# Four masks, a split fold and two queues: one edit set at the seam between a graph kernel's second and third layer

## The chip, the cores and the metric

The kernel runs on one core of one Trainium2 chip. The metric is the device time of one launch in microseconds (us). The kernel before took 700.03 us (median of three executions, 698.61 to 701.37).

## What is computed

Four pre-norm graph layers over 4096 nodes with 64 features. `adj` is a dense 4096 by 4096 float32 matrix with many zeros. Each layer is `x = x + L(relu(layernorm(x)), adj)`:

```
layer 0:  1 - 0.1 h - 0.01 sum(h * (adj @ h))
layer 1:  two hops  h = tanh([adj @ h, h] @ W[k])
layer 2:  w @ (h @ weight) + bias;  w keeps the last 100 nonzeros of each
          row of adj, weighted 0.5 ** (distance from the row's last one)
layer 3:  MLP(h) + adj @ (h B^T) - rowsum(adj) * (h B^T)
```

## The kernel before

The work is five passes over `adj`: `L0`, `L1A` (first hop), `L1B` (second hop), `L2`, `L3`. Each pass has 8 chunks of 512 output nodes, and each chunk 16 blocks (`b` = 0 to 15) of 1024 columns. Two consecutive blocks are a pair, 1 MB, which is the unit of a load. 15 of the 64 pairs stay in `cache`; all others are loaded again in every pass into one of the six slots of `land`. Neighbouring passes run over the chunks in opposite orders or end on the chunk where the next begins, so that the pairs in the slots serve twice at a seam: the last chunk of `L1B` and the first of `L2` are the same.

TensorE (PE) does two float32 matmuls per block in `L0`, `L1A`, `L1B` and `L3` (line 1373). In `L2` it does, per block, a triangle matmul on a 0/1 mask (`triangle`, line 1408), which gives each entry's rank as an exponent, and three blocks later (`LAG`) the weighted sum (`weigh`, line 1424). VectorE (DVE) makes the masks six blocks ahead (`LEAD`; `mask`, line 1155). ScalarE (ACT) turns ranks into weights (`weights_out`, line 591), except for blocks 3 and 13 of a chunk, which DVE does (line 589). Row 127 of each mask pair is not made by DVE: a small DMA brings it from `counts` (`counts_for`).

The row sums of `adj`, needed in `L3`, are gathered on DVE beside the hops: blocks in `TOTALS` are added up (lines 1107, 1111), and at a chunk's last such block `fold_totals` transposes and reduces them in two halves (lines 1138, 1139), through the tile `tS`. The total of the last `L1B` chunk lies in the uS places that masks 6 and 7 of `L2` will use, so those masks, and the counts rows for them (`counts_for(3)`, on SyncE's queue), wait until it is folded (semaphore `folded`).

What is done with a finished chunk, its epilogue, is cut into stages, and each engine runs stage k after the block that a table names: `STAGES_L1A`, `STAGES_L1B`, `STAGES_L2`, and `QUICK` for a pass's first chunk, which closes the pass before. For a chunk of `L1B` the stages go: ACT copies the sums out (line 850); PE joins two halves (line 1267); DVE adds the hop's own term ("added", line 1007) into `tS`; ACT does tanh (line 865) into `natS`; DVE adds the residual and centres the rows (3: lines 1075, 978, 979); GpSimd (POOL) squares (line 769); DVE makes the variance (4: lines 984, 985); POOL makes the inverse root (line 762) and scales (line 772); DVE takes the relu (5: line 997), which gives `hS`; PE transposes ("turn", line 1236); ACT copies to `rowsT` (line 830); PE multiplies by the layer-2 weight (6: line 1289); ACT copies back (8: line 883); POOL splits the rows in high and low parts (lines 795, 797). SyncE sends one row of the low part to another tile (`left_rows_of`, line 651), and the last matmul of an `L2` chunk (line 1432) needs it.

In `L2` the epilogue is similar: PE joins (line 1254), DVE adds (line 1082), and after the relu PE transposes (line 1276), ACT evacuates to `rowsT` (line 830), PE multiplies (line 1286). `rowsT` is also stored in DRAM as `rows_transposed` for `L3`, by SyncE's queue (`keep_rows`, line 656), and ACT doesn't overwrite `rowsT` before this store has landed (`hT_out`).

SyncE's queue runs in order. It carries all the loads of `adj`, each behind waits for the slot's last users, and between them the small DMAs: `after_masks` decides behind which load each goes. At the start of `L2`:

```
if p == L2 and c == 0:
    counts_for(2)
    sp.wait_ge(left_out, 16 * NC)
    left_over(0)
    left_over(1)
    counts_for(3)
```

After the last chunk of `L3`, `finish` runs three stages once more: ACT copies the sums (line 850), PE joins (line 1267), DVE adds the side term (line 1097), ACT's queue stores.

## Time and profile before

| | us |
|---|---|
| three executions | 698.61, 700.03, 701.37 |
| the profiled execution, its own time | 700.7 |
| its span, first to last instruction's end | 698.9 |
| PE busy | 668.3 (96%) |
| DVE busy | 469.6 (67%) |
| ACT busy | 192.5 (28%) |
| POOL busy | 114.2 (16%) |

The profile is one execution. A duration of an instruction is its own; "idle before" is the time in which its engine did nothing, with what ended that. PEld is the weight load of PE, which lies under the matmul before it. SPq and ACTq rows are the issues of DMAs. Of a DMA the time from issue to landing is given where the profile has it.

In time the passes lie as follows: `L0` to about 195 us, `L1A` to 311, `L1B` to 426.7, `L2` to 562, `L3` to the end.

### The profile page before, as it was taken

The page shows a single profiled execution, that of the slowest core. Times are in us where ns is not written, and L with a number is a line of the kernel's source. Part 1 is how long each engine was busy: PE and PEld are TensorE (multiplying, and loading weights), DVE is VectorE, ACT ScalarE, POOL GpSimd, SP SyncE. Part 2 cuts the span into 40 slices and gives each one's busy share as a digit, 9 for nine tenths or more (in the row PEclk, how much of TensorE's full clock was granted, in tenths as well). Part 3 has the DMA queues.
Part 4 walks back from the last instruction along what each step waited for, and adds up shares of the span by engine and source line. Part 5 has one row for each costly group of instructions (what it writes and reads, how often), then busy time and mean ns, then how long its engine had stood idle before and what let it go on. Part 6 is the DMA issues. An engine that isn't in the chain of part 4 may idle for free.

```text
span 698.9 us, 10418 instructions
## 1 busy us (share of the span) xinstructions
PE 668.3 (96%) x3811; PEld 270.2 (39%) x3824; DVE 469.6 (67%) x813; ACT 192.5 (28%) x296; POOL 114.2 (16%) x132
## 2 busy tenths in 40 slices
PE   3999999999999999999999998899999999999997
PEld 1434433334433333333344443444444443333332
DVE  7777767777899999996888888899989810000000
ACT  1101111011111001101111116899998811111111
POOL 4110011110200000001222223222332211211111
PEclk9999999999999999999999999999999999999999
DMA  8999999998589999959999983999999479999992
GB/s 347 422 410 411 413 412 409 418 414 335 190 329 388 420 422 419 415 206 402 384 406 420 419 368 134 362 378 408 414 414 412 191 263 341 417 415 418 417 419 98
DMA packets 42098, 256.51 MB, mean 367 GB/s; under 512 B 5120, under 2 KB 11264, under 8 KB 11840
## 3 DMA queue, kind: packets, MB, share of 16 engines
q1 hardware_dynamic: 38712, 252.85, 89.6%
q10 hardware_dynamic: 3336, 3.00, 1.5%
q8 instruction: 31, 0.51, 0.3%
q14 instruction: 19, 0.16, 0.1%
HBM read 252.28 MB, written 3.54 MB: 366 GB/s over the span
## 4 chain that ended last, share of the span: by engine, by line
PE 53%; DMA 20%; DVE 19%; POOL 4%; issue 3%; ACT 0%; SPq 0%; DVEq 0%; ACTq 0%; POOLq 0%
PE accA L1373 37%; DMA cache<-adj_blocks 10%; DVE uS L1111 8%; DMA land<-adj_blocks 6%; PE accA L1424 4%; PE work L1408 4%; DVE uS L1155 3%; POOL rstd L762 2%; DMA rows_transposed<-rowsT 2%; PE work L1391 1%; PE work L1336 1%; POOL tS L772 1%; PE accA L1342 1%; PE work L1267 1%; PE work L1304 1%
## 5 line engine op out<-in xcount | busy, mean ns | idle before, releaser
L1373 PE MATMUL accA<-land,X 128*64 128x512 f32 x1568 | 374.1, 598 | 13.6 <-DVE X L1197 11.3
L1373 PEld LDWEIGHTS accA<-land,X 128*64 128x64 f32 x1568 | 110.6, 137 | 193.7 <-issue 166.9
L1155 DVE TENSOR_SCALAR uS<-land 128x1024 bf16<-128x1024 f32 (+1 forms) x196 | 134.5, 730 | 30.1 <-DMA land<-adj_blocks 28.4
L1111 DVE TENSOR_TENSOR uS<-uS,land 128x512 f32<-128x512 f32 x178 | 125.2, 704 | 9.6
L1373 PE MATMUL accA<-cache,X 128*64 128x512 f32 x480 | 120.1, 598 | 2.6 <-DMA cache<-adj_blocks 2.6
L591 ACT ACTIVATE wS<-work 128x1024 uint16<-128x1024 f32 x114 | 109.2, 1037 | 8.8 <-PE work L1408 8.7
L769 POOL TENSOR_TENSOR hS<-tS 128x256 f32<-128x256 f32 x24 | 23.5, 978 | 400.5 <-DVE tS L979 400.5
L1097 DVE TENSOR_TENSOR zS<-uS,work 128x256 f32<-128x256 f32 x8 | 3.4, 421 | 123.1 <-PE work L1267 106.9
L1408 PE MATMUL work<-uS,triA 128*128 128x512 bf16 x248 | 74.4, 380 | 2.2 <-DVE uS L1155 1.8
L1424 PE MATMUL accA<-wS,X 128*128 128x512 bf16 x251 | 74.7, 379 | 0.3
L850 ACT ACTIVATE accS<-accA 128x512 f32<-128x512 f32 x32 | 19.1, 598 | 177.3 <-PE accA L1373 165.5
L1373 PEld LDWEIGHTS accA<-cache,X 128*64 128x64 f32 x480 | 35.0, 138 | 59.4 <-issue 54.8
L1391 PE MATMUL work<-uS,later 128*64 128x512 bf16 x256 | 49.1, 379 | 0.0
L1155 DVE TENSOR_SCALAR uS<-cache 128x1024 bf16<-128x1024 f32 (+1 forms) x60 | 39.8, 686 | 7.1 <-DMA cache<-adj_blocks 6.9
L762 POOL TENSOR_TENSOR rstd<-var,power 128x4 f32<-128x4 f32 (+1 forms) x25 | 34.0, 1360 | 34.7 <-DVE var L985 34.7
L1424 PEld LDWEIGHTS accA<-wS,X 128*128 128x128 f16 x256 | 25.0, 98 | 30.0
L1408 PEld LDWEIGHTS work<-uS,triA 128*128 128x128 bf16 x256 | 23.8, 101 | 26.3 <-DVE uS L1155 5.0
L1111 DVE TENSOR_TENSOR uS<-uS,cache 128x512 f32<-128x512 f32 x46 | 31.8, 691 | 2.5
L1391 PEld LDWEIGHTS work<-uS,later 128*64 128x64 bf16 x256 | 16.4, 110 | 35.5 <-issue 27.1
L997 DVE TENSOR_SCALAR hS<-tS 128x256 f32<-128x256 f32 x24 | 10.0, 416 | 27.1 <-POOL tS L772 27.1
L830 ACT ACTIVATE rowsT<-work 128x256 f32<-128x256 f32 x15 | 5.8, 384 | 70.0 <-PE work L1236 70.0
L782 POOL TENSOR_TENSOR uS<-X,rowsum 128x256 f32<-128x256 f32 x8 | 4.9, 613 | 100.4 <-DMA xin<-x_rows 78.4
(109 smaller groups left out, 417.4 us busy)
## 6 DMA issues: line engine op xcount, KB each, us to landing
land<-adj_blocks SPq DMA_DIRECT2D x221, 1024.0 KB, 10.3
cache<-adj_blocks SPq DMA_DIRECT2D x15, 1024.0 KB, 16.7
xin<-x_rows ACTq DMA_DIRECT2D x8, 128.0 KB, 7.6
out_rows<-zS ACTq DMA_DIRECT2D x8, 128.0 KB, 6.9
uS<-counts ACTq DMA_DIRECT2D x60, 4.0 KB
x_rows<-zS SPq DMA_DIRECT2D x7, 128.0 KB, 11.4
rows_transposed<-rowsT SPq DMA_DIRECT2D x7, 128.0 KB, 8.6
wS<-rows_transposed SPq DMA_DIRECT2D x7, 128.0 KB, 8.5
```

The lines of the kernel that those rows point to most:

```text
L591: ops.activation(w, of, ACT.Relu).then_inc(w_ready, 1)
L762: nc.gpsimd.tensor_tensor(out[:, 0:ntile], of[:, 0:ntile], power[:, 0:ntile], ALU.pow)\
L769: nc.gpsimd.tensor_tensor(hS[:, :], tS[:, :], tS[:, :], ALU.mult).then_inc(rows_squared, 1)
L772: nc.gpsimd.tensor_tensor(rows4(tS), rows4(tS), spread(rstd[:, 0:4]), ALU.mult).then_inc(rows_scaled, 1)
L850: last = nc.scalar.activation(accS[:, :], accA[:, c % 2, :], ACT.Copy)
L997: nc.vector.tensor_scalar(to, tS[:, :], 0.0, float(np.sqrt(D)), ALU.max, ALU.mult).then_inc(h_ready, 1)
L1111: nc.vector.tensor_tensor(total, total, of[:, i * W:(i + 1) * W], ALU.add)\
L1155: nc.vector.tensor_scalar(masks(p, c, b)[0:rows, :], block_of(p, c, b)[0:rows, :], 0.0, None, ALU.not_equal)\
L1373: last = nc.tensor.matmul(accA[k * D:(k + 1) * D, c % 2, :], tile(X[p % 2], TQ * q + k), of[:, k * W:(k + 1) * W], start=(b == 0), stop=(b ...
L1391: last = nc.tensor.matmul(spare[k * D:(k + 1) * D, c % 2, :], later[:, NT - t:NT - t + D], masks(L0, c, b)[:, k * W:(k + 1) * W], start=(b ...
L1408: last = nc.tensor.matmul(work[:, 2 * (n % TRI_PAIRS) + k, :], triA[:, :], masks(L2, c, b)[:, k * W:(k + 1) * W], start=True, stop=True)
L1424: last = nc.tensor.matmul(accA[:, c % 2, :], tile16(TQ * q + k), weights(n)[:, k * W:(k + 1) * W].bitcast(BF16), start=(b == 0 and k == 0) ...
```

## The change

1. DVE makes masks 0 to 3 of `L2`'s first chunk in the last chunk of `L1B`, after blocks 10, 12, 13 and 14 (`MASKS_AHEAD`).
2. At the start of `L2`, DVE's order is: mask 4, "added", mask 5, stage 3, first half of the fold, variance, second half of the fold, sum of the two parts. Before it was: masks 0 and 1, both halves and the sum, "added", masks 2 and 3, stage 3, masks 4 and 5, and the variance after the first block. The last fold goes through `zS` in place of `tS`.
3. PE does the join of the last `L1B` chunk after the second triangle of `L2`, no longer ahead of the first. The other quick stages come one or two blocks earlier.
4. In `L1A` "added" and tanh come one block earlier; in `L1B` the relu (5) comes after block 11, not 10.
5. The store of `rowsT` is issued by ACT right behind the copy that fills it, and no longer by SyncE.
6. The end of the kernel is done in two halves, each with its own copy, join, add and store.

```diff
+MASKS_AHEAD = {10: 0, 12: 1, 13: 2, 14: 3}
...
-STAGES_L1A = {1: 2, "added": 4, "tanh": 6, "hop": 8, "hopped": 10}
+STAGES_L1A = {1: 2, "added": 3, "tanh": 5, "hop": 8, "hopped": 10}
...
-STAGES_L1B = {1: 3, "added": 5, "tanh": 6, 3: 7, 4: 8, 5: 10, "turn": 12, "turned": 13, 6: 14, 8: 15}
+STAGES_L1B = {1: 3, "added": 5, "tanh": 6, 3: 7, 4: 8, 5: 11, "turn": 12, "turned": 13, 6: 14, 8: 15}
...
-         L2: {"tanh": 0, 4: 0, 5: 2, "turn": 8, "turned": 9, 6: 10, 7: 10, 8: 11,
-              "row sums": 14},
+         L2: {"tanh": 0, "join": 1, 5: 1, "turn": 7, "turned": 7, 6: 9, 8: 9,
+              "row sums": 12},
...
 def last_stages(before):
-    return [(k, before) for k in SUM_STAGES]
+    return [("last " + k, before) for k in SUM_STAGES]
...
+        def last_nat(h):
+            return (nat, tr)[h][:, 0:2 * D]
+
+        def last_half(t, h):
+            return t[:, h * 2 * D:(h + 1) * 2 * D]
...
-            def keep_rows(c):
-                sp.wait_ge(tr_evac, tr_no(L2, c) + 1)
-                sp.dma_start(hT_d[ch(L2, c)], rowsT[:, :]).then_inc(hT_out, 16)
...
-                if issued["keep"] < NC - 2 and g >= PAIRS * (issued["keep"] + 2) + 2:
-                    keep_rows(issued["keep"])
-                    issued["keep"] += 1
...
                     rows_transposed(p, c)
+                    if p == L2 and c < NC - 1:
+                        act.wait_ge(tr_evac, tr_no(p, c) + 1)
+                        act.dma_start(hT_d[ch(p, c)], rowsT[:, :]).then_inc(hT_out, 16)
...
+                if at == "last sums":
+                    act.wait_ge(intra_done, c + 1)
+                    act.wait_ge(swept, sweep_no(p, c) + 1)
+                    act.wait_ge(nat_done, nat_no(p, c))
+                    for h in range(2):
+                        nc.scalar.activation(accS[:, h * CH:(h + 1) * CH], accA[:, c % 2, h * CH:(h + 1) * CH], ACT.Copy)\
+                            .then_inc(acc_evac, 1)
+                if at == "last store":
+                    for h in range(2):
+                        act.wait_ge(nat_evac, nat_no(p, c) + 1 + h)
+                        act.dma_start(last_half(chunk(out, ch(p, c)), h), last_half(zS, h)).then_inc(rows_out, 16)
...
+                if (p, c) == (L1B, NC - 1) and b in MASKS_AHEAD:
+                    mask(L2, 0, MASKS_AHEAD[b])
...
-                for h in range(2):
+                by = zS if (p, c) == (L1B, NC - 1) else tS
+                for h in halves:
                     at = (2 * k + h) * 8
-                    L(nc.vector.transpose(tS[:, :], totals(k)[:, h * CH:(h + 1) * CH]))
+                    L(nc.vector.transpose(by[:, :], totals(k)[:, h * CH:(h + 1) * CH]))
...
                 if p == L2 and c == 0:
-                    for b in range(2):
-                        mask(p, c, b)
-                    fold_totals(L1B, NC - 1)
-                    nc.vector.tensor_tensor(part_sums, part_sums, more_sums, ALU.add).then_inc(folded, 1)
+                    mask(p, c, len(MASKS_AHEAD))
                     epilogue("added", before)
-                    for b in range(2, 4):
+                    for b in range(len(MASKS_AHEAD) + 1, LEAD):
                         mask(p, c, b)
                     epilogue(3, before)
-                    for b in range(4, LEAD):
-                        mask(p, c, b)
+                    fold_totals(L1B, NC - 1, halves=(0,))
+                    epilogue(4, before)
+                    fold_totals(L1B, NC - 1, halves=(1,))
+                    nc.vector.tensor_tensor(part_sums, part_sums, more_sums, ALU.add).then_inc(folded, 1)
...
-                if p != L2 and at == ("sums" if p == L3 else 1):
+                if p != L2 and at == ("sums" if p == L3 else "join" if (p, c) == (L1B, NC - 1) else 1):
```

PE's "last sums" waits for each half of ACT's copy, joins it with eight matmuls into `last_nat(h)`, and DVE's "last result" adds each half as it is done.

## Rows read from the trace of the kernel before

**Rows 1.** The page: GB/s moved by DMA in 40 slices of the span.

```profile
GB/s 347 422 410 411 413 412 409 418 414 335 190 329 388 420 422 419 415 206 402 384 406 420 419 368 134 362 378 408 414 414 412 191 263 341 417 415 418 417 419 98
```

**Rows 2.** Windows: length, busy PE, PEld, DVE, ACT, POOL, clock, DMA, GB/s.

```profile
335.20:413.70 78.50, 76.50 (x483) 33.26 (x481) 65.48 (x121) 8.91 (x20) 18.44 (x25) 1.00 1.01 413
...
426.75:449.93 23.18, 18.59 (x118) 7.94 (x120) 20.43 (x38) 19.69 (x24) 7.93 (x8) 1.00 0.83 305
449.93:465.92 15.99, 15.60 (x79) 7.93 (x80) 13.90 (x23) 14.10 (x17) 3.97 (x4) 1.00 0.99 379
...
530.10:547.30 17.20, 15.88 (x78) 7.70 (x79) 15.11 (x26) 13.90 (x18) 3.94 (x4) 1.00 1.01 416
```

**Rows 3.** Timeline, first hop: start, duration, engine, line, idle before.

```profile
202.96 0.68 DVE L1060 SCALAR_TENSOR_TENSOR countS<-lowS,rowsT 32x512 uint16<-32x512 f32 x1
...
204.23 0.71 PE L1304 MATMUL work<-wts,rowsT 64*128 64x128 f32 x8 [0.88 <-ACT rowsT L865]
```

**Rows 4.** Timeline of PEld: the join in chunks of the second hop.

```profile
320.16 0.14 PEld L1267 LDWEIGHTS work<-wts,accS 128*64 128x64 f32 x2 [0.28 <-issue]
...
335.23 0.14 PEld L1267 LDWEIGHTS work<-wts,accS 128*64 128x64 f32 x2 [0.28 <-issue]
...
413.67 0.17 PEld L1267 LDWEIGHTS work<-wts,accS 128*64 128x64 f32 x2 [0.26 <-issue]
```

**Rows 5.** Second hop: PE's and DVE's waits (total, times, longest), and loads.

```profile
PE work L1236 <- DVE hS L997: 2.6, 6, 0.6
...
DVE hS L997 <- POOL tS L772: 12.7, 7, 1.8
...
L753 SPq DMA_DIRECT2D land<-adj_blocks x31: 327/328/437, 335.8 to 408.8; - x31
...
DMA to landing us min/median/max: 6.8/9.3/11.6
```

**Rows 6.** Timeline of the second hop's last chunk and of L2's first.

```profile
422.63 0.29 DVE L997 TENSOR_SCALAR hS<-tS 128x256 f32<-128x256 f32 x1 [1.81 <-POOL tS L772]
422.84 1.41 DVE L1111 TENSOR_TENSOR uS<-uS,land 128x512 f32<-128x512 f32 x2
...
425.69 1.29 DVE L1155 TENSOR_SCALAR uS<-land 127x1024 bf16<-127x1024 f32 x2
...
428.75 0.22 SPq L634 DMA_DIRECT2D uS<-counts  x1
...
434.38 0.59 PE L1408 MATMUL work<-uS,triA 128*128 128x512 bf16 x2
...
449.62 0.37 PE L1432 MATMUL accA<-lowS,later 32*128 32x512 bf16 x1 [1.57 <-DMA later<-X]
```

**Rows 7.** Loads in L2 at 456:471 and 520:535; a DVE wait.

```profile
DMA to landing us min/median/max: 7.1/8.4/10.3
...
DMA to landing us min/median/max: 12.6/14.7/15.7
...
545.91 1.30 DVE L1155 TENSOR_SCALAR uS<-land 127x1024 bf16<-127x1024 f32 x2 [1.08 <-DMA land<-adj_blocks]
551.43 0.42 DVE L1082 TENSOR_TENSOR zS<-X,accA 128x256 f32<-128x256 f32 x1 [0.69 <-PE accA L1254]
```

**Rows 8.** Stores of rows: L2, then L3 (issue to landing last); ACT and PE.

```profile
rows_transposed<-rowsT SPq DMA_DIRECT2D x5, 128.0 KB, 12.0
...
out_rows<-zS ACTq DMA_DIRECT2D x5, 128.0 KB, 6.9
...
543.53 0.38 ACT L830 ACTIVATE rowsT<-accA 128x256 f32<-128x256 f32 x1 [2.74 <-DMA rows_transposed<-rowsT]
544.06 0.68 PE L1286 MATMUL accA<-wts,rowsT 128*128 128x128 f32 x4 [1.09 <-ACT rowsT L830]
```

**Rows 9.** Timeline of the end.

```profile
694.67 0.60 ACT L850 ACTIVATE accS<-accA 128x512 f32<-128x512 f32 x1 [11.41 <-PE accA L1373]
...
696.59 0.34 ACTq L614 DMA_DIRECT2D out_rows<-zS  x1
```

More of the change, by code:

```diff
@@ L679, in _ @@
             LEFT_ROWS_AT = {NC - 3: 1, NC - 2: 3, NC - 1: 7}
-            issued = {"keep": 0, "left": 2, "left rows": NC - 3}
+            issued = {"left": 2, "left rows": NC - 3}
             def step(p, c, before, before2):
@@ L697, in step @@
                     after_masks(PAIRS * NC - 1)
-                    keep_rows(NC - 2)
                 if p == L0:
@@ L948, in finish @@
                     epilogue(k, e)
-                act.wait_ge(rows_out, 16 * 2 * NC)
+                act.wait_ge(rows_out, 16 * (2 * NC + 1))
             for g in range(1, PRO_GROUPS):
@@ L1091, in epilogue @@
                     side = sideS[:, (c % 2) * CH:(c % 2 + 1) * CH]
+                    if at == "last result":
+                        dve.wait_ge(side_ready, c + 1)
+                        rows_written()
+                        for h in range(2):
+                            dve.wait_ge(nat_done, nat_no(p, c) + 1 + h)
+                            nc.vector.tensor_tensor(last_half(zS, h), last_half(side, h), last_nat(h), ALU.add)\
+                                .then_inc(nat_evac, 1)
                     if at == "result":
@@ L1124, in main, with fold_totals @@
                     weights_out(dve, nc.vector, c, b)
-            def fold_totals(p, c):
+            def fold_totals(p, c, halves=(0, 1)):
                 k = ch(p, c)
@@ L1257, in epilogue @@
                         last.then_inc(nat_done, 1)
-                if p != L2 and at == ("sums" if p == L3 else 1):
+                if at == "last sums":
+                    nat_free(nat_no(p, c, 0))
+                    for h in range(2):
+                        pe.wait_ge(acc_evac, NC * p + c + 1 + h)
+                        for j, at, half in pieces(4)[4 * h:4 * h + 4]:
+                            last = nc.tensor.matmul(last_nat(h)[half, (j % 2) * D:(j % 2 + 1) * D], accS[:, at:at + D], wt("join"),
+                                                    start=True, stop=True)
+                        last.then_inc(nat_done, 1)
+                    return
+                if p != L2 and at == ("sums" if p == L3 else "join" if (p, c) == (L1B, NC - 1) else 1):
                     nat_free(nat_no(p, c, 0))
@@ L1435, in step @@
             def step(p, c, before, before2):
-                for k, e in early_stages(p, c, before, before2):
-                    epilogue(k, e)
                 s = NC * p + c
```

4 lines of the change are left out of this document (1 added, 3 removed).

## The prediction

> **What bounds the kernel now.** I read the waits first, then windows by pass, then the timeline of the seam at 427 us, then the landing times of the loads. PE is busy 96% of the span, so only what PE waits for, or what sets its pace, can be gained. Three resources run close together. In the second hop the DMA share is 1.01 and 413 GB/s are moved [rows 2], against a best slice of 422 [rows 1]: about 2% is left there. In the first hop DMA is as full (420 to 422 in its slices [rows 1]). In L2 it starts empty (0.83, 305 GB/s in the first chunk) and is full at the end (1.01, 416) [rows 2]; a load there lands 8.4 us after its issue early on and 14.7 us late [rows 7]. The backlog grows while PE, at 16.0 us a chunk, isn't hurt yet. The reader should keep this in mind: what PE gains before L2 must be matched by the loads in L2.
>
> Places where PE loses time, and which the edits touch:
>
> - Second hop: PE waits for the relu `hS` six times, 2.6 us [rows 5]. The join comes 15.07 us after the one before in the first chunk, which has no such wait, and then 78.44 us for five chunks (335.23 to 413.67), 15.69 each [rows 4]. So a chunk loses 0.62, more than the wait shown, since the weight loads ahead are no longer hidden. What makes `hS` late is DVE's own loop: it stands idle 12.7 us in seven chunks, 1.8 each, for POOL's scaling [rows 5], with sums still to do.
> - First chunk of L2: 23.18 us against 15.99 for the next [rows 2], with 1.57 us of wait for the small DMA ahead of line 1432 [rows 6].
> - The chunk 530.1 to 547.3: 17.20 us [rows 2]. ACT waits 2.74 us until the earlier store of `rowsT` has landed, PE then 1.09 [rows 8].
>
> **Part by part.** All in us, gains negative.
>
> *Relu after block 11 (second hop).* The sums of block 11 (1.41 [rows 6]) move into DVE's idle 1.81, and the relu still starts when POOL is done, at 422.63 in the row. DVE's loop falls from 15.65 to about 14.24, under PE's 15.07. So each of the five chunks gains 0.62: -3.1. If loads hold it back, less: 31 loads were issued from 335.8 to 408.8 and land 6.8 to 11.6 later, median 9.3 [rows 5]. The last one, pair 1 of the last chunk, is thus in by about 418.1 (415.6 to 420.4). DMA can come forward by some 1.5 at most (2% of 78.5).
>
> *Four masks in that chunk.* Mask 0 is made after block 10 and needs just that pair 1. DVE's queue stands still until it has landed, and behind it are the sums of block 11 and the relu. The old relu ended at 422.92 [rows 6] with PE waiting 0.6 for it; with PE 3.1 earlier, the turn would want `hS` at 419.2. With the landing at 418.1 it is ready at 418.1 + 0.65 (a mask is half of line 1155's 1.29 for two [rows 6]) + 1.41 + 0.29 = 420.5. PE waits 1.3, where it waited 0.6. I take 0.8 off the gain: second hop -2.3, bounds -1.0 (landing as late as the row allows) and -3.7 (all waits gone).
>
> *Start of L2.* PE needn't wait for ACT's copy nor for masks 0 to 5: three triangles run at once. But masks 6 and 7 and their counts rows wait for the fold, and the fold moves behind "added", stage 3 and the variance. Counted from the second hop's end T (426.75 before [rows 2]): join done T + 1.6 (two triangles and the join), "added" 2.1 (0.42, as line 1082 has for the same size [rows 7]), mask 5 2.7, stage 3 (three such instructions and a wait for tanh) 4.1. Both halves of the fold and the sum took from the end of the first two masks, 426.98, to the issue at 428.75 [rows 6], so half a fold takes 0.85: 5.0. The variance waits for POOL's square, an estimated 1.0 (the idle 1.81 holds two POOL steps [rows 6]): 5.9, half a fold and the sum 6.8. SyncE's `counts_for(3)` was issued at 428.75 [rows 6], which is T + 2.0; now it goes at T + 6.8. It lands some 2 later, and triangle 6 starts at T + 8.8; before it was 434.38 - 426.75 = T + 7.6 [rows 6]. So PE stands idle before triangle 6 and is 1.2 behind. What gives it back: the turn, layer-2 weight and row split come one and two blocks earlier, the row leaves for line 1432 at about T + 16.5 and is in before PE is there. From triangle 6 to line 1432 PE took 449.62 - 1.57 - 434.38 = 13.7 before [rows 6], with some waits for ACT in it that I put at 0.7, so 13.0 now: T + 21.8 against 449.62 - 426.75 = T + 22.9. Sum -1.0, rounded; bounds +0.5 (counts 1.5 later) and -1.6 (nothing but the 1.57 of wait).
>
> *What is queued behind that wait.* `counts_for(3)` holds SyncE's queue, and behind it are all the loads for L2's second chunk. They were first issued right behind it, at 429.1; with T 2.3 earlier (424.4) they now start at 431.5, three at once. So PE comes 3.3 earlier to the second chunk and the loads start 2.4 later. They catch up, since before they were spaced by waits for slots: I count a pace of 2.6 each from the first landing, 436.4, which puts the sixth at 449.4, and about 1.3 more from later gaps that close. Loads in L2 end up some 2.2 earlier than before, PE wants to be 3.3 and later 4.8 earlier.
>
> *Store of rowsT by ACT.* It no longer stands behind 1 MB loads in SyncE's queue. There it took 12.0 to land, the same size from ACT's queue in L3, with the loads at 417 GB/s, 6.9 [rows 8]. It is also issued at once. The chunk at 530.1 falls from 17.2 to the usual 16.0, 0.3 of start-up apart: -1.5 (bounds 0 and -1.5). The cost: ACT waits for its own copy and issues, some 0.4 per chunk. It lies in the time in which ACT has nothing to do (busy 14.10 of 15.99 in a chunk [rows 2]), next to block 13, whose weights DVE makes. Without that cover it would be 7 x 0.4 = 2.8.
>
> The Trainium skill, "DMA: Bandwidth & Descriptors", section "Queues, rings and completion order", says that each DMA engine takes turns between the queues it has work for. By that the store alternates with the loads, as 6.9 beside 12.0 suggests. The same page, "Issuing engines are not separate DMA queues", says that a second issuer saves only issue time, which speaks against any more bandwidth; by it the loads gain nothing here and the sum stays.
>
> *Give-back in L2.* At 545.91 DVE waits 1.08 for a load and, five masks and a weight later, still has 0.69 of idle before line 1082 [rows 7], from where the chain to `hS` and the turn is tight. So the loads may come 0.7 later against PE than they did, and no more. With loads 2.2 earlier, PE can be 2.9 earlier at the end of L2, where the edits alone would give -2.3 - 1.0 - 1.5 = -4.8. Give-back +1.9, bounds 0 (DMA recovers all) and +3.5 (loads not earlier at all).
>
> *First hop.* "Added" was never late there but once: PE waited 0.88 at 204.23 [rows 3]. ACT's tanh was then released by line 1060 (202.96 to 203.64), which shares `rowsT` and stays where it is, with as much DVE work ahead as before. 0; at most +0.4, as the sums of a block end 0.41 later.
>
> *The end.* From 694.67 to the last store's issue at 696.59 is 1.92 [rows 9]. In halves, copy, join and add overlap: the second half's add is half as long and the join of the first lies under the second copy, at two short copies of 0.38 [rows 8] for one of 0.60. -0.3; bounds +0.1 and -0.5. The last store is half as big; the row bounds what that is worth by the 2.3 from its issue to the span's end, most of which I expect to stay. The Trainium skill, same page, "Anatomy of one DMA", fits a DMA from GpSimd's queue by about 2.0 and its bytes at 436 GB/s, which is 2.3 for these 128 KB, as in the trace; by that the smaller store would bring an estimated 0.15 more than my sum has.
>
> **Sum.** -2.3 - 1.0 - 1.5 + 1.9 + 0 - 0.3 = -3.2. The profiled execution had 700.7 with a span of 698.9, so 697.5 and 695.7. The median stands 0.7 below that execution: 700.0 - 3.2 = 696.8.
>
> **Rivals.**
>
> 1. *Loads keep up* (chance 0.25). For it: in the first 40 us of L2 the loads had gaps, and the stores leave SyncE's queue. Against: 416 GB/s at the end. Then no give-back: 700.0 - 4.8 - 0.3 = 694.9.
> 2. *The late fold costs what the masks bring* (0.20). Loads aren't earlier at all, give-back +3.5, or the last chunk of the second hop waits for pair 1: -4.8 + 3.5 - 0.3 = -1.6: 698.4.
> 3. *Slower: counts behind the store in ACT's queue* (0.07). The counts rows for blocks 6 and 7 of the next chunk are issued after block 15, right after the store, and their triangle runs seven blocks later, at 16.0 a chunk about 7.0. If they come only after the store has landed, it decides whether that takes more than 7. With the 6.9 of rows 8 it just doesn't. At 9.5 it costs 2.5 in each of six chunks, +15: 700.0 - 3.2 + 15 = 712. From 8 us on the change is slower.
> 4. *My forecast*: 0.48.
>
> **How the numbers follow.** About 0.5% (3.5 us) is what a measurement of this kernel can tell from no change. My case lies at 696.8 with its own range 695.5 to 698.0, so it is split by 696.5: 0.2 faster, 0.28 same. Faster is 0.25 + 0.2 = 0.45, same 0.28 + 0.20 = 0.48, slower 0.07. The range goes from 694.3 (rival 1 with somewhat more of the hop) to 699.0 (rival 2 with the bounds of the fold).
>
> **What would show it.** Joins in the second hop 15.07 apart; no PE wait on `hS` except in the last chunk, and there a DVE wait for a load at mask 0; `counts_for(3)` some 6.8 after the hop's end and PE idle before triangle 6; no wait at line 1432; no ACT wait for `rows_transposed`; chunks of L2 that grow from 16.0 at the start to more than 16.3 at the end with DVE waits for loads of 2 us and more. Wrong would be: full 16.0 to the end (rival 1), hop chunks still at 15.6, or waits of triangles for counts.

## The result and the profile after

The changed kernel takes 702.97 us (median of seven runs, 701.88 to 704.47) beside 700.03 for the kernel before; the ratio is 1.0044, its 95% interval 1.0029 to 1.0059. It is slower by 2.9 us. The forecast was 696.8 with a range up to 699.0, so the result lies outside it. Of the cases in the forecast only rival 3 (0.07) lay above, at 712. The profiled run took 704.47 with a span of 702.6, which is 3.7 more than the span before.

The lines of the page of the changed kernel that answer to the table of before, and the granted clock in 40 slices of the span:

```profile
span 702.6 us, 10422 instructions
...
PE 669.2 (95%) x3810; PEld 272.3 (39%) x3824; DVE 471.9 (67%) x814; ACT 193.0 (27%) x297; POOL 120.4 (17%) x132
...
PEclk9999999999999999999999999899999999999999
```

PE has the same work. It is busy 0.9 longer (669.2 beside 668.3) and idle 2.8 longer; where it is busy longer, its clock was low, as the second chunk of L2 below shows. One slice of the clock, from 439 to 457 us, is not full; before, none was short. POOL is busy 6.2 us longer with the same instructions.

The windows of the changed kernel, in the columns of [rows 2] (length, busy PE, PEld, DVE, ACT, POOL, clock, DMA share, GB/s): five chunks of the second hop, L2 from the end of the hop to line 1465 (which is line 1432 of before), the next chunk, and the slow chunk late in L2.

```profile
334.84:412.07 77.23, 76.48 (x483) 33.77 (x481) 67.03 (x120) 8.90 (x20) 23.61 (x25) 1.00 1.01 413
425.76:450.71 24.95, 17.97 (x115) 7.73 (x118) 17.95 (x34) 19.92 (x24) 7.42 (x8) 0.97 0.70 284
450.71:469.17 18.46, 18.26 (x79) 8.84 (x80) 13.58 (x22) 13.34 (x16) 3.97 (x4) 0.86 0.88 332
533.53:550.48 16.95, 15.87 (x79) 7.98 (x80) 15.39 (x24) 14.41 (x18) 4.18 (x4) 1.00 1.02 416
```

The hop gained 1.2 over five chunks where the prediction wanted 3.1. The first chunk of L2 took 24.95; from the same point, the end of the hop, to the same matmul it was 22.84 before. The second chunk has the same work as before and takes 18.46 instead of 16.01, at a clock of 0.86. Cut at the same events, the two spans part like this:

| stretch | before | after | change |
|---|---|---|---|
| start to the first join of the second hop (J) | 320.16 | 319.42 | -0.74 |
| J to the end of the second hop | 106.59 | 106.34 | -0.25 |
| end of the hop to the left row of L2's first chunk | 22.84 | 24.95 | +2.11 |
| second chunk of L2 | 16.01 | 18.46 | +2.45 |
| six more chunks of L2 | 96.22 | 96.67 | +0.45 |
| from there to the first `intra` matmul of L3 | 17.39 | 17.43 | +0.04 |
| rest | 119.69 | 119.37 | -0.32 |

The first row needs care: 0.72 of the 0.74 are there already at 189 us, before any edited stage has run, and in the changed kernel and those below J lies between 317.25 and 319.42. So stretches are compared from J on.

Timeline of the changed kernel at the seam (start, duration, engine, line, and in brackets the idle time before and what ended it):

```profile
427.44 0.42 DVE L1024 TENSOR_TENSOR tS<-wS,accA 128x256 f32<-128x256 f32 x1 [1.77 <-issue]
...
429.63 0.44 DVE L1165 STREAM_TRANSPOSE zS<-uS 128x256 f32<-128x256 f32 x1
...
431.57 0.42 DVE L1166 TENSOR_REDUCE wts<-zS 128x8 f32<-128x256 f32 x1
432.02 0.22 SPq L646 DMA_DIRECT2D uS<-counts  x1
...
432.34 0.83 SPq L756 DMA_DIRECT2D land<-adj_blocks  x2
...
433.43 0.59 PE L1441 MATMUL work<-uS,triA 128*128 128x512 bf16 x2 [2.12 <-DMA uS<-counts]
...
433.93 0.87 SPq L756 DMA_DIRECT2D land<-adj_blocks  x2
...
437.84 1.54 SPq L756 DMA_DIRECT2D land<-adj_blocks  x2
...
441.80 0.60 SPq L663 DMA_DIRECT2D later<-X  x1
...
446.09 0.59 PE L1457 MATMUL accA<-wS,X 128*128 128x512 bf16 x2
...
450.74 0.58 PE L1465 MATMUL accA<-lowS,later 32*128 32x512 bf16 x1 [4.06 <-DMA later<-X]
```

And the six loads that are issued from 432 to 440, from issue to landing:

```profile
DMA to landing us min/median/max: 4.7/10.1/11.9
```

Read it from the top. DVE is idle for 1.77 before "added", since it waits for the join; the fold, which before the change stood in that place, comes only at 429.63 and ends at 431.99. The counts rows leave at 432.02, 6.3 after the hop's end (before: 2.0 [rows 6]). Two things follow from that one issue. PE is idle for 2.12 before triangle 6. And the loads of the second chunk, which stand behind the counts rows in SyncE's queue, leave in a bunch: the first four, whose slots are free, in 2.1 us, all six in 6.7. Before, the six went out over 12.3 us, from 429.1 to 441.4, and landed in 4.9 to 9.3; now it is up to 11.9. The small DMA with the last row is issued at 441.80 behind them, when four of them are still on their way, and is in at about 450.7. Before, it was issued at 445.32 with two on their way, and was in at about 449.6. PE has finished its last block at 446.7 and waits 4.06. During this wait, at 449.04, the chip's clock for TensorE falls to its 1.2 GHz level (0.5 in the record) for 6.83 us, and PE does the first part of the second chunk at half speed. The mean granted clock is 0.994 or 0.995 in all seven executions of the changed kernel, and the fall accounts for that.

The last chunk of the second hop in the changed kernel, where mask 0 is made ahead:

```profile
419.13 0.69 DVE L1182 TENSOR_SCALAR uS<-land 127x1024 bf16<-127x1024 f32 x1
419.30 1.38 POOL L765 TENSOR_TENSOR rstd<-var,power 128x4 f32<-128x4 f32 x1 [1.16 <-DVE var L1002]
419.74 1.41 DVE L1135 TENSOR_TENSOR uS<-uS,land 128x512 f32<-128x512 f32 x2
420.76 0.85 POOL L775 TENSOR_TENSOR tS<-tS,rstd 128x256 f32<-128x256 f32 x1
421.65 0.29 DVE L1014 TENSOR_SCALAR hS<-tS 128x256 f32<-128x256 f32 x1 [0.50 <-POOL tS L775]
...
422.09 0.66 PE L1260 MATMUL work<-wts,hS 128*64 128x128 f32 x8 [1.20 <-DVE hS L1014]
```

Mask 0 waited for no load, which the prediction had feared. PE's wait of 1.20 came from POOL, which was late instead. Without the masks ahead (e4_no_seam below) it is 0.96 in the same place, against 0.58 before the change, so most of the lateness isn't the masks'.

### The profile page after: what moved, and what is told of

Read it like the earlier page. It is cut to its first block, busy times and chain, and to the rows that moved or that the text cites. A ratio compares the mean times of both kernels' runs of the same rounds, so it can differ in the third digit from the quotient of the medians.

```text
span 702.6 us, 10422 instructions
## 1 busy us (share of the span) xinstructions
PE 669.2 (95%) x3810; PEld 272.3 (39%) x3824; DVE 471.9 (67%) x814; ACT 193.0 (27%) x297; POOL 120.4 (17%) x132
## 4 chain that ended last, share of the span: by engine, by line
PE 54%; DMA 22%; DVE 15%; POOL 4%; issue 4%; ACT 0%; SPq 0%; DVEq 0%; ACTq 0%; POOLq 0%
PE accA L1406 38%; DMA cache<-adj_blocks 10%; DMA land<-adj_blocks 10%; DVE uS L1135 7%; PE work L1441 4%; PE accA L1457 4%; POOL rstd L765 2%; DVE uS L1182 2%; PE work L1424 1%; DMA later<-X 1%; PE work L1369 1%; PE work L1300 1%; POOL tS L775 1%; PE accA L1375 1%; PE work L1260 1%
## 5 line engine op out<-in xcount | busy, mean ns | idle before, releaser
L1135 DVE TENSOR_TENSOR uS<-uS,land 128x512 f32<-128x512 f32 x178 | 127.5, 716 | 9.3
```

The source lines that it names most:

```text
L1135: nc.vector.tensor_tensor(total, total, of[:, i * W:(i + 1) * W], ALU.add)\
```

## The experiments

Fourteen kernels, each timed in five rounds against the kernel before on the same chip. The last three columns are from the profiled run of each: from J to the left row of L2's first chunk, the second chunk, and the six after it. Before has 129.43, 16.01, 96.22; the changed kernel 131.29, 18.46, 96.67. The comparisons were made on several chips, where the kernel before had medians of 699.5 to 700.0, so a difference between two medians of this table is good to some tenths; the ratios allow for that.

| kernel | median | ratio to before | J to left row | 2nd chunk | six more |
|---|---|---|---|---|---|
| e4_no_seam | 697.31 | 0.9966 (0.9955 to 0.9978) | 127.25 | 16.00 | 96.65 |
| e11_late_fold | 704.58 | 1.0057 (1.0037 to 1.0078) | 133.09 | 18.49 | 96.12 |
| e9_fold_first | 697.63 | 0.9968 (0.9955 to 0.9980) | 127.94 | 16.01 | 96.87 |
| e12_fold_first_kept | 696.76 | 0.9949 (0.9929 to 0.9970) | 127.26 | 16.00 | 96.50 |
| e1_left_by_act | 700.08 | 1.0004 (0.9991 to 1.0016) | 128.76 | 16.00 | 98.52 |
| e2_counts_by_act | 698.71 | 0.9987 (0.9974 to 1.0000) | 130.47 | 15.99 | 96.20 |
| e8_both_by_act | 699.81 | 0.9994 (0.9978 to 1.0010) | 131.27 | 15.99 | 96.22 |
| e3_filler | 701.69 | 1.0031 (1.0019 to 1.0044) | 132.76 | 15.99 | 95.72 |
| e13_fold_first_left_by_act | 697.64 | 0.9964 (0.9949 to 0.9979) | 128.18 | 16.00 | 96.59 |
| e5_store_by_act | 699.45 | 0.9998 (0.9985 to 1.0011) | 129.20 | 16.01 | 96.90 |
| e6_relu11 | 698.47 | 0.9983 (0.9969 to 0.9997) | 127.47 | 16.00 | 97.21 |
| e14_turn_later | 693.66 | 0.9902 (0.9881 to 0.9923) | 124.69 | 16.00 | 96.34 |
| e15_masks_ahead_turn_later | 696.06 | 0.9945 (0.9928 to 0.9962) | 126.04 | 16.01 | 96.12 |
| e16_changed_turn_later | 701.15 | 1.0012 (0.9995 to 1.0028) | 129.23 | 18.63 | 96.68 |

### Without the seam edits: e4_no_seam

The kernel before with the hop orders, the store by ACT and the two-part end; masks, fold, join and `QUICK[L2]` as before.

> The kernel before with only the three edits away from the seam: the relu after block 11 in the second hop and added/tanh a block earlier in the first, the store of rowsT by ACT, and the two-part end. Theory A: nothing of the loss, since the masks, the fold and the counts are where they were; second hop 1.2 faster over five chunks, the chunk at 530 about 0.5 to 1.4 faster, the end 0.3: 698.0 to 699.0, clock 1.00. If these edits carry the loss (ACT's queue with the store in it, or the relu): 701 or more.

697.31, faster than before. By the ratios the rest of the change brings 2.4 us; the seam edits (masks ahead, early join, late fold, earlier stages) turn 0.9966 into 1.0044 and so cost 5.5. The kernel is faster than the 698.0 to 699.0 expected.

### The late fold alone: e11_late_fold

```diff
                     for b in range(2):
                         mask(p, c, b)
-                    fold_totals(L1B, NC - 1)
-                    nc.vector.tensor_tensor(part_sums, part_sums, more_sums, ALU.add)...
                     epilogue("added", before)
...
                     for b in range(4, LEAD):
                         mask(p, c, b)
+                    fold_totals(L1B, NC - 1)
+                    nc.vector.tensor_tensor(part_sums, part_sums, more_sums, ALU.add)...
```

This is e4_no_seam with the fold moved, and through `zS`, as in the change.

> The kernel with edits 4 to 6 alone (697.3), with one more edit: the fold goes behind the added sum, stage 3 and masks 4 and 5 in VectorE's order; no mask is made ahead, and the stages of L2's start stay where they were. Theory A (the late fold alone makes the loss): counts rows at 5 us or more after the hop's end, PE idle 1.5 or more before triangle 6, loads in a bunch of four or more within 3 us, the one-row DMA late by 2 or more, and 701 to 703 in all. Theory B (the late fold hurts only together with the early masks and stages, since PE otherwise comes as late as the counts): 697 to 699.

704.58: 7.3 more than e4_no_seam (6.4 by the ratios), the slowest of all, and above the 701 to 703 of theory A. Timeline of this kernel:

```profile
433.39 0.22 SPq L640 DMA_DIRECT2D uS<-counts  x1
...
434.89 0.59 PE L1436 MATMUL work<-uS,triA 128*128 128x512 bf16 x2 [2.17 <-DVE uS L1174]
...
445.57 0.60 SPq L657 DMA_DIRECT2D later<-X  x1
...
452.26 0.58 PE L1460 MATMUL accA<-lowS,later 32*128 32x512 bf16 x1 [3.86 <-DMA later<-X]
```

The whole picture is there without any mask made ahead: counts late, PE idle before triangle 6 (what comes last there is mask 6, which waits for the fold too), the row late, a second chunk of 18.49.

### The fold first again: e9_fold_first and e12_fold_first_kept

The changed kernel with the order of the fold put back, all else kept:

```diff
                     mask(p, c, len(MASKS_AHEAD))
+                    fold_totals(L1B, NC - 1)
+                    nc.vector.tensor_tensor(part_sums, part_sums, more_sums, ALU.add)...
                     epilogue("added", before)
...
-                    fold_totals(L1B, NC - 1, halves=(0,))
                     epilogue(4, before)
-                    fold_totals(L1B, NC - 1, halves=(1,))
-                    nc.vector.tensor_tensor(part_sums, part_sums, more_sums, ALU.add)...
```

> The changed kernel with one thing put back: both halves of the fold and the sum stand ahead of the added sum in VectorE's order (as before the change), while four masks are still made ahead and the stages come early. Theory A (the late fold is the seam's whole loss): VectorE is idle 1.8 us there, waiting for the join, so the fold costs nothing; counts rows go out some 2 us after the second hop's end and not 6.3, PE has no idle time ahead of triangle 6 (2.1 less), the loads are no longer issued in a bunch, the one-row DMA lands within 3 us, PE waits at most 1 for it and the clock stays at 1.0: 696.5 (695.5 to 697.5), level with the kernel that has no seam edits (697.3) or just under it. Theory B (the early masks and the earlier stages cost by themselves, or the last row is late whatever the loads do): PE still waits 3 or more at the row and the time stays at 700 or above.

e9_fold_first transposes into `zS`, which still holds the kept rows of the last chunk until stage 3 has added them, so in this kernel the fold's values take their place and the rows of that chunk are lost. Its instructions and their order are those of e12_fold_first_kept, which folds through `tS` and keeps them.

> The changed kernel with the fold ahead of the added sum again, through the tile tS as before the change, so that the kept rows of the last chunk survive. Same operations, order and waits as the kernel with the fold first that gave 697.6: both theories expect 697.6 within 0.7, so that this is a repetition; more than 1.5 above it would mean that the tile matters.

697.63 and 696.76, so the place of the fold in VectorE's order is worth 5.3 and 6.2 us; from J to the first `intra` matmul it is 6.7 in the profiled runs (257.14 against 263.85). In the timeline of e12_fold_first_kept:

```profile
425.91 0.22 SPq L646 DMA_DIRECT2D uS<-counts  x1
...
426.23 0.83 SPq L756 DMA_DIRECT2D land<-adj_blocks  x2
...
440.21 0.60 SPq L663 DMA_DIRECT2D later<-X  x1
...
445.14 0.37 PE L1464 MATMUL accA<-lowS,later 32*128 32x512 bf16 x1 [1.32 <-DMA later<-X]
```

The six loads land in 4.8 to 8.8 here instead of 4.7 to 11.9, the row is issued with two of them on their way and needs less than 5 instead of 9, and no clock is lost. Theory A of e9_fold_first holds in mechanism; 697.63 is just above its range.

### What goes through the row and what through the loads: e1, e2, e8, e3

e1_left_by_act: the changed kernel, last one-row DMA by ACT after block 12.

```diff
+                if (p, c, b) == (L2, 0, 12):
+                    act.wait_ge(copy_used, copied_no(L1B, NC - 1, 1) + 1)
+                    act.dma_start(loS[4 * NC - 4:4 * NC, :], chunk(X[1], NC - 1)[LAST:P, :]...
```

> The changed kernel, but the last of the eight one-row transfers that line 1465 waits for is issued by ACT's queue (after block 12 of L2's first chunk) and not by SyncE's. Theory A (the row stands behind six loads in SyncE's queue, PE idles 4.06 us for it, and the granted clock then falls to half for 6.8 us): the row lands within 4 us of its issue at about 442.5, PE reaches line 1465 at 446.7 and doesn't wait, the clock stays at 1.00, L2's second chunk takes 16.0 and not 18.4; 4.1 + 2.4 less, of which L2's loads take back 1 to 3: 696.5 to 699.5 against 703.0. Rival B (the loads themselves, started 3.3 us later than before, set the end of L2, and the row only hides it): the row's wait goes but L2 ends no earlier, 701 to 703.

It was issued at 440.80 on the other queue and PE waits 1.54 in place of 4.06. The clock stays at 1.0 and the second chunk at 16.00, 700.08 in all: above the 696.5 to 699.5 of theory A and below the 701 of its rival. But the loads are as late as before the edit, and the six later chunks take 98.52, 1.85 more than in the changed kernel.

e2_counts_by_act: the counts rows of masks 6 and 7 by ACT, so that loads are not queued behind them.

```diff
-                    counts_for(3)
...
+                if (p, c, b) == (L2, 0, 5):
+                    act.wait_ge(folded, SUMMED - 1)
+                    act.dma_start(*counts_of(3)).then_inc(counts_in[3], 16)
```

> The changed kernel, but the counts rows for masks 6 and 7, which wait for the fold, are issued by ACT (after block 5) and not by SyncE, so that SyncE's loads aren't held behind the fold. Theory A: loads start at about 427 to 429 as slots come free, fewer stand ahead of the row, PE's wait at line 1465 falls from 4.1 to 1 or less and the clock may stay up: 697 to 700. Rival B (late loads): the same place gains, and more than in the run with the row on ACT's queue, 696 to 698. If neither the start of the loads nor the row matters: 703.

The first three loads leave at 422.66, 424.18 and 427.58, before the counts rows (431.05). PE waits 3.79 for the counts, longer than before: with loads already on their way it is 3.1 from their issue to PE's start, against 1.4 in the changed kernel, where the counts rows go first. Just after this wait the clock falls, for 3.41 us from 434.54 on. PE doesn't wait at all for the row, and the later chunks keep 96.20. 698.71. Freeing the loads brings more than freeing the row alone.

> The changed kernel with both small DMAs taken off SyncE's queue: counts rows of masks 6 and 7 by ScalarE after block 5, the last one-row DMA by ScalarE after block 12. Each alone gave 698.7 and 700.1. Theory A (two separate losses, one from loads held back, one from the row behind a bunch of loads): counts still wait for the late fold, PE waits 2 to 4 there, but neither the row nor the clock costs: 697.5 to 698.5. Theory B (L2 is bound by DMA at its end, and what PE gains at its start goes back): no better than the better of the two, 698.7 or 0.3 around it.

e8_both_by_act has both edits. 699.81 is not better than e2_counts_by_act; theory A wanted 697.5 to 698.5. The window over the first chunk of L2, from its profiled execution (701.36, the slowest of its twelve), shows what happened there:

```profile
426.50:450.53 24.03, 19.62 (x113) 8.25 (x114) 17.94 (x34) 18.30 (x23) 4.65 (x7) 0.86 0.79 286
```

PE waits 3.6 for the counts, and the clock falls right then, from 433.49 on for 6.83 us, inside this chunk. Removing the second wait did not remove the first. The twelve executions differ in how much clock they lost: the four with a mean clock of 0.995 took 699.57 to 701.36, the two with 0.999 took 697.49 and 697.86, inside theory A's range. So where the clock stayed up, theory A's time came; but the first wait alone is enough to bring the clock down in some executions, and the median contains that. Neither theory had this.

e3_filler puts 70 matmuls of 128x128 into PE's wait for the row; nothing uses their result.

```diff
+                        pe.wait_ge(nat_evac, nat_no(L1B, NC - 1, 1) + 1)
+                        pe.wait_ge(rowsum_ready, 1)
+                        for _ in range(70):
+                            nc.tensor.matmul(accA[:, 1, 0:P], triA[:, :], triA[:, :], start=True, stop=True)
                         pe.wait_ge(left_rows, 16 * NC)
```

> The changed kernel with 70 needless 128x128 matmuls on PE ahead of the wait at line 1465, into a bank that is free, so that PE is busy while it waits for the row. Theory A's second part (it is PE's idle time of 4 us that lets the granted clock fall to half): the row is as late as ever (about 450.7), but the clock stays at 1.00 and the second chunk of L2 takes 16.0: 2.4 less, 700.5. Rival (the clock falls for another reason): clock 0.99 as before and 703.0.

The window over its second chunk:

```profile
452.02:468.01 15.99, 15.66 (x79) 7.94 (x79) 13.58 (x22) 13.33 (x16) 3.97 (x4) 1.00 0.97 348
```

With PE kept busy the clock doesn't fall there, and the same chunk takes 15.99 instead of 18.46, though the dummies end only at 452.0, 1.3 after the row was in in the changed kernel. Net it is 1.3 faster, where 2.4 had been expected. In this execution the clock fell once before the edit, at 434.48 for 3.41 us, which put PE back by some 1.5, and the dummies with it. All six executions have a mean clock of 0.997 or 0.998, against 0.994 or 0.995 in all seven of the changed kernel. So 2.45 of the loss are the clock, and PE's idle time at the row brought this fall about.

> The changed kernel with the fold first and the last one-row DMA issued by ScalarE after block 12. Theory A (PE's 1.9 of wait at that row, which is left with the fold first, is worth its length): 696.0. Theory B (loads bind the end of L2, so what PE gains at its start goes back before its end): the wait goes away, the first left-row matmul starts at 445 instead of 446.8, and the time stays within 0.5 of 697.6.

e13_fold_first_left_by_act: e12_fold_first_kept and the edit of e1. 697.64, no gain: PE waits 1.0 at the row and 1.6 for weights before it, and from J it reaches the row no earlier. Once the fold is right, the row's queue is not a lever; theory A's 696.0 did not come.

### The other parts: e5_store_by_act and e6_relu11

The kernel before with the store alone:

```diff
-SyncE: keep_rows(c), called in after_masks and at L3's start
...
                     rows_transposed(p, c)
+                    if p == L2 and c < NC - 1:
+                        act.wait_ge(tr_evac, tr_no(p, c) + 1)
+                        act.dma_start(hT_d[ch(p, c)], rowsT[:, :]).then_inc(hT_out, 16)
```

> The kernel before with the store of the transposed rows on ScalarE's queue alone. Prediction: -1.5 before give-back, with 6.9 instead of 12.0 us from issue to landing: 698.3. Rival: the chunk that had waited for the store falls from 17.2 to 17.0 only, since a load is late there too, and the next one takes it back: within 0.3 of before, 699.4 or so.

699.45, ratio 0.9998. The store of `rowsT` lands in 7.0 now (median; 6.9 in the prediction), and ACT no longer waits for it. Yet the chunk falls only from 17.49 to 17.13, and the next rises from 14.56 to 15.43. The rows of e5_store_by_act in that stretch:

```profile
528.37 1.29 DVE L1149 TENSOR_SCALAR uS<-land 127x1024 bf16<-127x1024 f32 x2 [1.29 <-DMA land<-adj_blocks]
...
537.11 1.29 DVE L1149 TENSOR_SCALAR uS<-land 127x1024 bf16<-127x1024 f32 x2 [0.36 <-DMA land<-adj_blocks]
...
540.22 0.41 PE L1270 MATMUL accA<-wts,hS 128*128 128x128 f32 x2 [1.00 <-DVE hS L991]
...
540.73 0.38 ACT L821 ACTIVATE rowsT<-accA 128x256 f32<-128x256 f32 x1 [1.42 <-PE accA L1270]
541.14 0.35 ACTq L872 DMA_DIRECT2D rows_transposed<-rowsT  x1
...
545.48 1.29 DVE L1149 TENSOR_SCALAR uS<-land 127x1024 bf16<-127x1024 f32 x2 [1.07 <-DMA land<-adj_blocks]
```

ACT's idle is now ended by PE, that is by the turn, which waits for `hS`, which waits for masks, which wait for loads: DVE's waits for loads in the last two chunks are 2.7 (1.4 before), 1.29 and 0.36 of them ahead of this turn and 1.07 in the chunk after it. The wait has only changed its name. Rival 3 of the prediction (counts behind the store in ACT's queue) did not show: no triangle waits for counts in these chunks.

The kernel before with the hop orders alone:

```diff
-L1A: {1: 2, "added": 4, "tanh": 6, ...}    L1B: {... 4: 8, 5: 10, "turn": 12, ...}
+L1A: {1: 2, "added": 3, "tanh": 5, ...}    L1B: {... 4: 8, 5: 11, "turn": 12, ...}
```

> The kernel before with the two hop orders changed alone (relu of the second hop after block 11, first hop one block earlier). Prediction's step: second hop -3.1 without the masks, joins 15.07 apart, so 697.4 after give-back. Rival (POOL's variance step takes 1.4 instead of 1.0 when it runs beside VectorE's sums, and the new order waits for the join instead): joins 15.44 apart, -1.0 to -1.3 at the hop's end, and 698.7 to 699.3 in all.

698.47, a little under the 698.7 to 699.3 of the rival. The joins stand 15.44 apart, not 15.07, as the rival had it. POOL's `rstd` in the second hop, first in the kernel before, in the changed one, and in e6_relu11 (count, then min/median/max of the duration in ns):

```profile
L762 POOL TENSOR_TENSOR rstd<-var,power x6: 1007/1009/1012, 326.6 to 405.0; 128x4 f32<-128x4 f32 x6
```

```profile
L765 POOL TENSOR_TENSOR rstd<-var,power x6: 1386/1388/1394, 325.8 to 403.0; 128x4 f32<-128x4 f32 x6
```

```profile
L762 POOL TENSOR_TENSOR rstd<-var,power x6: 1387/1388/1393, 324.8 to 402.0; 128x4 f32<-128x4 f32 x6
```

In the old order DVE was idle while POOL worked on the variance. In the new one DVE's sums run beside it, and each `rstd` takes 0.38 longer. That lies on the chain join, "added", square, variance, `rstd`, scale, relu, turn, and the chunk is just that much longer: 15.44 - 15.07 = 0.37. (PE's own waits at the turn show as 0.2 in three of the chunks.) That this chain, and not the loads, sets the 15.44 is shown by the next kernel.

The Trainium skill, "GPSIMD Engine Reference", section "Specifications", says that GpSimd's SBUF interfaces are shared with VectorE, with contention when a VectorE instruction has two SBUF inputs. The sums have two (`uS` and `land`), and the trace agrees in direction; it shows 0.38 of delay for one instruction.

### The turn one block later: e14, e15, e16

```diff
-L1B: ... 5: 11, "turn": 12, "turned": 13, 6: 14, 8: 15}
+L1B: ... 5: 11, "turn": 13, "turned": 14, 6: 15, 8: 15}
```

> The kernel with edits 4 to 6 alone (697.3), with the turn, its copy and the split of the second hop's chunks one block later. Theory A (joins stand 15.44 apart since PE, at the turn of block 12, waits 0.4 in each chunk for a chain that begins at the join of block 3: join, added, square, variance, rstd 1.39, scale, relu): with a block more the wait goes away, joins stand 15.07 apart, the hop ends 1.8 earlier, and 695.5 to 697 in all, what loads in L2 take back included. Theory B (loads set 15.44): joins stay 15.4 apart, with waits for loads in VectorE, and the time stays at 697.3.

e4_no_seam with this: 693.66, ratio 0.9902, the best kernel here: 5.9 under the kernel before and 9.3 under the changed one, between medians. It is below the 695.5 to 697 of theory A. The medians differ by 3.7 from e4_no_seam; in the profiled runs 2.9 lie between J and L3, and 1.7 before J, where the two kernels don't differ in an edited stage. The joins stand 15.07 apart in all six intervals, and `rstd` still takes 1.39, so loads did not set 15.44; the chain did. Counted from J, PE ends the hop 3.5 earlier than in e4_no_seam (some 0.6 of it because stage 6 now stands behind the last block), reaches the left row 2.6 earlier, and keeps that: the last six chunks take 96.34 (96.65 there, 96.22 before).

> The changed kernel with the fold ahead of the added sum (696.8) and the turn, its copy and the split of the second hop's chunks one block later; against the kernel with the later turn and no seam edits (693.7) it has the four masks ahead, the early join and the earlier stages of L2's first chunk. Theory A (masks ahead cost some 0.4 at the turn of the last hop chunk and give as much back at L2's start): within 0.7 of 693.7. Theory B (as in the prediction, masks ahead and early stages bring 1 us at the start of L2): 692.7 or less. Theory C (the split of the last chunk, now a block later, makes the one-row DMA late, which the early stages were to avoid): PE waits 2 or more there and 695 or more.

e12_fold_first_kept with the later turn: 696.06, 2.4 slower than e14_turn_later between medians (3.0 by the ratios). In the profiled runs 2.06 lie before J, where the two don't differ in an edited stage, so that part isn't explained. From J on the masks ahead and the early stages cost 1.35 up to the left row, where PE waits 2.4 (0.5 in e14_turn_later). Theory C comes nearest; theory B, gain from the early masks, is wrong.

> The changed kernel with nothing else than the turn, its copy and the split of the second hop's chunks one block later; the fold stays late. Theory A (the later turn gains its 3 to 4 us in the hop, in front of the seam, and the seam costs what it did): joins 15.07 apart and 699 to 700. Theory B (PE comes earlier to waits that are set by VectorE and POOL, so part of the gain goes into them): joins 15.07 apart, PE idle before triangle 6 and at the row by 1 to 2 more than in the changed kernel (2.1 and 4.1), and 701 or more.

The changed kernel with the later turn: 701.15. Theory A had 699 to 700. Its timeline:

```profile
429.79 0.59 PE L1441 MATMUL work<-uS,triA 128*128 128x512 bf16 x2 [2.23 <-DMA uS<-counts]
...
447.11 0.58 PE L1465 MATMUL accA<-lowS,later 32*128 32x512 bf16 x1 [4.07 <-DMA later<-X]
```

Joins are 15.07 apart. The waits before triangle 6 and at the row, 2.2 and 4.1, are those of the changed kernel, and the second chunk of 18.63 is nearly so. But of the 3.4 by which the hop ends earlier, counted from J, only 2.1 are left at the left row and 1.9 at L3. Some 0.6 of the difference is stage 6, which now stands behind the last block. And PE waits 0.7 for a mask at the first triangle of L2, where it waited 0.2 at most; the join stands behind that, and all that hangs on the join. The counts rows leave 7.5 after the hop's end, not 6.3. Against e14_turn_later the seam edits cost 7.5 between J and L3, where they cost 6.6 against e4_no_seam. So theory B has the time, and its mechanism in part: PE comes earlier to a wait that DVE sets, though not to one of the two that it named.

## Why the prediction was wrong, step by step

*Start of L2* is the step that failed. It said "the row leaves for line 1432 at about T + 16.5 and is in before PE is there". It left at T + 16.0 and PE was there at T + 20.9 (T + 21.8 had been forecast); the row came at T + 25.0. The issues were right within 0.6: counts at T + 6.3 (6.8) and the row; triangle 6 ran at T + 7.7 (8.8). What was missing is what the step *What is queued behind that wait* had already written down: loads that leave together. Its list of landings was used for the give-back, but not for the small DMA behind them in the same queue. By that list the sixth load landed at 449.4, and PE was to be at the row at 424.4 + 21.8 = 446.2; a row that lands with that load would have cost some 3, not nothing (it measured 4.06). The step's -1.0 measured +2.11, outside its bounds (+0.5), and the clock added 2.45, a term the sum did not have at all. [rows 6] showed the danger: the same DMA was already late by 1.57 with loads spaced out.

*Relu after block 11.* The sums do move into DVE's idle time, but the five chunks gained 1.2 and not 3.1. The term took POOL's durations from rows in which DVE was idle; the edit is what ends that idleness. DVE's loop was not the only one that PE's 15.07 had to cover; the chain through POOL was the second, 0.37 longer, and one block more of slack (e14_turn_later) removed just that. The first interval, which had none of the old wait (15.07), became 15.43 too.

*Four masks in that chunk.* -2.3 with the relu, measured -0.25, beyond the bound of -1.0. The mechanism named (mask 0 waits for a load) did not occur. The turn waited 1.20 all the same, since POOL was slower: `rstd` took 1.38, which is the relu's order again (1.39 in e4_no_seam, with a wait of 0.96), and the scale 0.85 beside a mask and sums (0.61 there). From J to the hop's end the masks cost 0.25 against e4_no_seam.

*Store of rowsT by ACT.* -1.5, measured 0 (e5_store_by_act, 0.9985 to 1.0011), which was the lower bound. The latency was right (7.0); the chunk had a second cause, a load, just behind the first. The term was also more than its own rows give: from 17.2 to 16.0 are 1.2.

*Give-back in L2.* +1.9, measured about nothing: e14_turn_later reaches the left row 4.7 earlier from J than before, and its next six chunks take only 0.12 longer. Rival 1 was right on that. The store's gain did go to loads that were late, but their lateness does not grow with PE's lead, as the forecast had it. What gave back was something else: e1_left_by_act loses 1.85 there, since its loads were held up by the fold and its PE was not.

*First hop* 0 and *The end* -0.3 were right: -0.02 from 189 us to J, and -0.32. All kernels with the two-part end take 119.37 to 119.45 from the first `intra` matmul on, those without it 119.58 to 119.69.

The sum was wrong by 6.9 against the span (3.7 for -3.2). Start of L2 has 3.11 of it, the clock 2.45, hop and masks 2.05; the rest of L2 has 0.09, since +0.49 was measured and -1.5 and +1.9 cancel to +0.4; the end has -0.02 and the stretch before J -0.74. Two errors hid each other there: a gain and a give-back, neither of which came as forecast.

Of the rivals, 2 named the late fold, and priced it as loads that come no earlier: 698.4. 3 had the sign, by a mechanism that isn't there. No two of the masks ahead, the early join and the earlier stages were run apart, so what each of them costs or brings by itself stays open.

## What to carry to other kernels

When an edit delays an issue in a DMA queue, list everything behind it, and not only the big loads: they leave in a bunch, and a 1 KB transfer behind them lands when they do. A step that fills one engine's idle time changes the durations of the engine that it now runs beside; take the price from rows where both are busy. And where a wait disappears from a chain, look for the chain of nearly the same length before booking the gain: here one block more of slack for the turn brought 1.6 to 2.9 us between J and L3 in three pairs of kernels, and the seam edits with the fold put back 0.15 at best (they cost 1.1 with the later turn).

## What the runs showed of the hardware

- A 1 KB DMA issued from SyncE's queue lands about when the 1 MB load issued before it does: 450.7 beside 450.96 in the changed kernel, 452.2 beside 452.30 in e11_late_fold, 445.1 beside 445.20 in e12_fold_first_kept. In the kernel before, e4_no_seam, e6_relu11 and e14_turn_later it was some 1.2 earlier than that load, in e9_fold_first and e15_masks_ahead_turn_later 0.3 later. From ACT's queue it took 6.4 with four loads on their way (e1_left_by_act) and 5.8 with three (e13_fold_first_left_by_act), so another queue helps but is no bypass. The Trainium skill, "DMA: Bandwidth & Descriptors", section "Queues, rings and completion order", says that an engine takes turns between queues and works off one queue's ring in order; the rows agree in direction with both halves: in its own queue the row came with the load ahead of it, from the other queue 2.6 before it (447.2 beside 449.79).
- In the second hop POOL's `rstd` has two durations with hardly any spread: 1.01 with DVE idle, 1.39 beside DVE's sums. In L2, beside masks, which read one tile, it took up to 1.77. The cast of line 798 took 0.73 in six chunks of the second hop (0.40 in the kernel before) and 2.19 beside four masks in L2 (2.06 before).
- TensorE's clock fell to 1.2 GHz in the seam for 6.83 or 3.41 us during or just after waits of PE of 4.06, 3.86, 4.07, 3.79 and 3.6 us in the profiled runs, and not after 2.4 or 1.5. But e3_filler shows a fall of 3.41 at 434.48, after 2.2 of waiting, where the changed kernel with 2.12 has none; the length of one wait doesn't decide it alone. What does was not separated. The kernel before is not free of it either: in the comparison with e5_store_by_act, 6 of 35 executions of the kernel before have a mean clock of 0.997 or 0.998 and took 701.3 on average, the others, at 0.999 or 1.000, 699.6. The difference of 1.7 is what 3.41 us at half speed would cost, an estimate, since these executions have no trace.
